# Another column order for the residual xT, and three bias-row copies given to GpSimd

## The reference, cut to what matters

```
x = x + L0(_gn(x))   # layer norm over c; q, k, v, gate; attention over n (16 x 16) for each (a, b), 8 heads;
                     # o = att @ v * sigmoid(gate);  o @ Wo + bo
x = x + L1(_gn(x))   # zn = one norm over everything;
                     # a = sigmoid(lin(zn, W_ga)) * lin(zn, W_la), b likewise with W_gb, W_lb
                     # k = einsum('bitc,bjtc->bijc', a, b); kn = one norm over everything
                     # sigmoid(lin(zn, W_go)) * lin(kn, W_lo)
```

## Time and profile before

| what | value |
|---|---|
| median of three executions | 345.86 us (345.86, 346.84, 344.46) |
| the profiled execution | 347.44 us, of which the span of instructions 345.5 us |
| TensorE's granted clock, mean over the span | 0.897 of full speed |
| busy: PE, PEld, DVE, ACT, POOL | 72%, 44%, 75%, 63%, 57% of the span |
| pipeline of the first block | about 37 to 263 us |
| scalars of the second norm | 263 to 269 us |
| second block up to the final stage | 269 to 320 us |
| final stage and store | 320 to 345.5 us |
| first small matmul behind the wait for B1 (`chsum`) | 264.09 us |
| GpSimd's first `z1_norm`, after 12.9 us idle | 268.69 us |
| first DMA into `bbd[0]` | 282.57 us |
| ScalarE's scaling of unit 7 ends | 328.77 us |

### The profile page before, as it was taken

One profiled execution on the slowest core, in us unless ns is written; L12 is line 12 of the kernel. 1 busy time (PEld: TensorE's weight loads), 2 busy tenths in 40 slices (PEclk: granted clock), 3 DMA queues, 4 the chain that ended last, 5 costly groups with the idle time before them and its releaser, 6 DMA issues.

```text
span 345.5 us, 7455 instructions
## 1 busy us (share of the span) xinstructions
PE 249.6 (72%) x2982; PEld 151.5 (44%) x2982; DVE 258.1 (75%) x466; ACT 217.3 (63%) x392; POOL 195.8 (57%) x169
## 2 busy tenths in 40 slices
PE   0056965599779779679679669769864599998724
PEld 0046342377347346346346347346531145554223
DVE  4985789766797898898898895899796764431972
ACT  4635787389569669669579669468341447567512
POOL 6890564659885896886877843434840862000620
PEclk9995799658998999999999998998997599999856
DMA  7100122013031031031031022100000014667207
GB/s 248 31 0 30 33 63 63 0 39 86 0 93 32 2 92 35 1 93 32 5 88 34 30 64 55 40 0 3 2 2 0 1 30 93 169 183 199 62 0 243
DMA packets 34893, 19.66 MB, mean 57 GB/s; under 512 B 21228, under 2 KB 31788, under 8 KB 34860
## 3 DMA queue, kind: packets, MB, share of 16 engines
q1 hardware_dynamic: 34860, 19.20, 20.7%
HBM read 8.71 MB, written 6.29 MB: 43 GB/s over the span
## 4 chain that ended last, share of the span: by engine, by line
DVE 41%; PE 36%; ACT 14%; issue 7%; DMA 1%; POOL 1%; DVEq 0%; ACTq 0%
PE PS L1126 31%; DVE t_sb L876 6%; DVE nmax L892 5%; DVE S_sb L896 4%; DVE og L869 4%; DVE gn_part L964 3%; DVE sums L820 3%; ACT u_sb L593 2%; ACT PP L623 2%; DVE Z L1113 2%; DVE Z L1117 2%; PE PS L1390 2%; ACT t_sb L607 2%; PE PS L1195 1%; DVE st L830 1%
## 5 line engine op out<-in xcount | busy, mean ns | idle before, releaser
L1126 PE MATMUL PS<-znT,A_bd 128*128 128x512 f16 x192 | 46.9, 387 | 11.8 <-DVE t_sb L876 10.5
L427 POOL TENSOR_TENSOR S_sb<-S_sb,rden 128x512 f32<-128x512 f32 x32 | 35.5, 1133 | 27.7 <-DVE rden L838 27.7
L876 DVE TENSOR_TENSOR t_sb<-PS,t_sb 128x512 f16<-128x512 f32 x64 | 41.1, 683 | 8.6 <-ACT t_sb L607 8.6
L607 ACT CAST t_sb<-PS 128x512 f16<-128x512 f32 x64 | 36.6, 611 | 15.0 <-PE PS L1126 13.5
L613 ACT ACTIVATE S_sb<-S_sb 128x512 f32<-128x512 f32 x32 | 20.2, 631 | 31.8 <-DVE S_sb L896 31.8
L1126 PE MATMUL PS<-zbd,t_sb 128*128 128x64 f16 x768 | 28.9, 199 | 13.6 <-DVE t_sb L876 12.8
L433 POOL TENSOR_TENSOR PP<-S_sb,PP 128x512 f16<-128x512 f32 x28 | 31.8, 1158 | 12.0 <-ACT PP L601 12.0
L1126 PEld LDWEIGHTS PS<-zbd,t_sb 128*128 128x128 f16 x768 | 26.0, 102 | 25.1 <-DVE t_sb L876 16.7
L1126 PE MATMUL PS<-PP,Z 128*128 128x128 f16 x512 | 34.6, 236 | 0.2 <-DVE PP L850 0.2
L593 ACT COPY u_sb<-PS 128x512 f32<-128x512 f32 x64 | 33.7, 626 | 1.6 <-PE PS L1126 1.4
L1126 PEld LDWEIGHTS PS<-znT,A_bd 128*128 128x128 f16 x192 | 16.9, 99 | 40.6 <-DVE t_sb L876 23.9
(11 more groups left out here) (198 smaller groups left out, 529.5 us busy)
## 6 DMA issues: line engine op xcount, KB each, us to landing
Z<-zn_dram SPq DMA_DIRECT2D x64, 64.0 KB, 2.8
x_tok<-in_x SPq DMA_DIRECT2D x4, 512.0 KB, 5.6
zn_dram<-zn_tok SPq DMA_DIRECT2D x8, 256.0 KB, 2.0
zbd<-znT SPq DMA_DIRECT2D x32, 64.0 KB, 2.0
k_dram<-og SPq DMA_DIRECT2D x4, 512.0 KB, 3.6
th<-k_dram SPq DMA_DIRECT2D x16, 128.0 KB, 2.7
out_x<-u_sb SPq DMA_DIRECT2D x4, 512.0 KB, 3.3
PP<-u_sb SPq DMA_DIRECT2D x8, 128.0 KB, 2.4
```

The costliest lines, as they stand in the source:

```text
L427: nc.gpsimd.tensor_tensor(P, P, bcast(rden[:, 32 * k:32 * k + 32], 2, N), ALU.mult).then_inc(p_nrm, 1)
L607: nc.scalar.copy(t_sb[:, HI, :, h], bank_tg(h)[:, :].rearrange("p (q i) -> p q i", i=N)).then_inc(t_hi, 1)
L876: nc.vector.tensor_tensor(t_sb[:, LO, :, h], bank_tg(h)[:, :].rearrange("p (q i) -> p q i", i=N), t_sb[:, HI, :, h], ALU.subtract).then_in ...
L1126: return nc.tensor.matmul(o, l, r, start=start, stop=stop)
```

## The change

The columns of xT are kept in the order (b, n, f) instead of (b, f, n): for one n, the eight values of f are neighbours, and for two n sixteen values are. What follows from it in the code: ScalarE's copy of the transposed x (L692) no longer permutes; the output projection reads `og` permuted, its innermost step being 16 f32 (64 bytes); the two reductions for the statistics run over two axes with an innermost step of one; `z1_norm` reads with other strides of f; and the final additions (L552, L1117) read runs of sixteen. Apart from this, the three copies into `B1` go from VectorE to GpSimd, between its two clears of `bbd`, with waits on `bbd_z` and on `wprep2`.

```diff
--- before.py
+++ after.py
@@ -142,7 +142,7 @@
                .rearrange("p (n c j) -> p n c j", n=4, j=L), x_tok[:, :, :, :].rearrange("p a b c -> p (a b c)").rearrange("p (n c j) -> p n c j", n=4, j=L)]
         gt = [S_sb[:, 4 * k:4 * k + 4].rearrange("p q a n -> p (q a n)")
               .rearrange("p (m c a) -> p m (c a)", a=A2, m=2) for k in range(3)]
-        x1_nfb = xT[:, :].rearrange("p (b f n) -> p b n f", f=A4, n=N)
+        x1_nfb = xT[:, :].rearrange("p (b n f) -> p b n f", f=A4, n=N)
         k_sb = og[:, :, :].rearrange("p h c -> p (h c)")
         kT = th[:, :, :, :].rearrange("p k h c -> p (k h c)")
         tg = Z[:, :, :, :, :, :, :].rearrange("p r f k e d b -> p (r f k e d b)").bitcast(f32)
@@ -256,6 +256,7 @@
 
 
 
+        WPREP2 = 16 + 12 + 1 + 5 + 3
         LZ, LV = 7, 4
         LOOPS = (NS - 4) // 2
         UNITS = (0, 2, 4, 1, 3, 5, 6, 7)
@@ -461,7 +462,7 @@
         def z1_norm(engine, ops, g, done):
 
             for n in range(4 * g, 4 * g + 4):
-                ops.tensor_scalar(z1f[g % 2][:, :, n % 4], xT[:, :].rearrange("p (b f n) -> p f b n", f=A4, n=N)[:, :, :, n],
+                ops.tensor_scalar(z1f[g % 2][:, :, n % 4], xT[:, :].rearrange("p (b n f) -> p f b n", f=A4, n=N)[:, :, :, n],
                                   g2[:, 10, n:n + 1], g2[:, 11, n:n + 1], ALU.mult, ALU.add).then_inc(done, 1)
 
         def z1_low(engine, ops, g, done):
@@ -533,6 +534,13 @@
             for j in range(NS - 1, NS + 2):
                 pool_period(pool, j, j % 2, tail=j <= NS, LN=j < NS - 1)
             nc.gpsimd.memset(bbd[1].rearrange("p n c j -> p (n c j)"), 0.0).then_inc(bbd_z, 1)
+            pool.wait_ge(bbd_z, 1)
+            for r in range(3):
+                pool.wait_ge(wprep2, WPREP2 - 3 + r)
+                row = slice(32 * r, 32 * r + 1)
+                nc.gpsimd.tensor_copy(B1[row, :, :, :, :].rearrange("p k m d e -> p (k m d) e"),
+                                      bcast(b1_s[row, r].rearrange("p k m d -> p (k m d)"), 2, A2)).then_inc(wprep2, 1)
+            pool.wait_ge(wprep2, WPREP2)
             pool.wait_ge(u_mm, 8 * NS)
             nc.gpsimd.memset(bbd[0].rearrange("p n c j -> p (n c j)"), 0.0).then_inc(bbd_z, 1)
 
@@ -689,8 +697,7 @@
                 nc.scalar.copy(x_perm[:, :, e], x_tok[:, e]).then_inc(xp_ok, 1)
             def xT_copy(i):
                 act.wait_ge(xT_mm, i + 1)
-                nc.scalar.copy(xT[:, COLS * i:COLS * i + COLS].rearrange("p (b f n) -> p b f n", f=A4, n=N),
-                               PS[2 + i % 2][:, :].rearrange("p (b n f) -> p b f n", f=A4, n=N)).then_inc(xT_ok, 1)
+                nc.scalar.copy(xT[:, COLS * i:COLS * i + COLS], PS[2 + i % 2][:, :]).then_inc(xT_ok, 1)
             xT_copy(0)
             act.wait_ge(gn_ok, 8)
             nc.scalar.activation(gn_r[:, :], gn_tmp[:, 2], ACT.Sqrt).then_inc(rsq, 1)
@@ -824,12 +831,12 @@
 
             dve.wait_ge(x1_ok, s + 1)
             nc.vector.tensor_reduce(st1[:, 0, bass.ds(s, 1)].rearrange("p s n -> p (s n)"),
-                                    xT[:, bass.ds(s * COLS, COLS)].rearrange("p (q n) -> p n q", n=N),
-                                    op=ALU.add, axis=AX.X).then_inc(x1_st, 1)
+                                    xT[:, bass.ds(s * COLS, COLS)].rearrange("p (b n f) -> p n b f", n=N, f=A4),
+                                    op=ALU.add, axis=AX.XY).then_inc(x1_st, 1)
             dve.wait_ge(x1_sq, s + 1)
             nc.vector.tensor_reduce(st1[:, 1, bass.ds(s, 1)].rearrange("p s n -> p (s n)"),
-                                    sqx[:, :].rearrange("p (q n) -> p n q", n=N),
-                                    op=ALU.add, axis=AX.X).then_inc(x1_st, 1)
+                                    sqx[:, :].rearrange("p (b n f) -> p n b f", n=N, f=A4),
+                                    op=ALU.add, axis=AX.XY).then_inc(x1_st, 1)
 
         def dve_reciprocal(dve, m, half):
             dve.wait_ge(p_sum, 4 * m + 2 * half + 2)
@@ -906,7 +913,6 @@
                                                op0=ALU.add, op1=ALU.add).then_inc(x1_ok, 1)
 
         WP1 = 3 + 4 + 1 + 1
-        WPREP2 = 16 + 12 + 1 + 5 + 3
 
         def dve_weights2(dve):
 
@@ -945,10 +951,6 @@
                     nc.vector.tensor_tensor(b1_r[:, r], rest, b1_s[:, r], ALU.subtract).then_inc(wprep2, 1)
                     n += 1
                     rest = b1_r[:, r]
-            for r in range(3):
-                row = slice(32 * r, 32 * r + 1)
-                nc.vector.tensor_copy(B1[row, :, :, :, :].rearrange("p k m d e -> p (k m d) e"),
-                                      bcast(b1_s[row, r].rearrange("p k m d -> p (k m d)"), 2, A2)).then_inc(wprep2, 1)
             assert n + 3 == WPREP2
 
         def zero(v):
@@ -1227,7 +1229,8 @@
         def pe_out(pe, s):
             for k in range(A2):
                 pe.wait_ge(o_ok, HP * s + k + 1)
-                last = mm(bank_w[D * k:D * k + D], Wo_h[:, :], og[:, k])
+                last = mm(bank_w[D * k:D * k + D], Wo_h[:, :],
+                          og[:, k].rearrange("p (b f i) -> p b i f", f=A4, i=N))
             last.then_inc(w_mm, 1)
 
         def pe_period(pe, j, par, half, B=True, A=True):
```

## The result

| | before | after |
|---|---|---|
| median of 19 executions | 345.2 us (343.12 to 347.61) | 341.35 us (338.05 to 344.65) |
| ratio | 1 | 0.9855, 95% interval 0.9825 to 0.9884 |
| profiled execution: span, mean granted clock | 345.5 us, 0.897 | 340.2 us, 0.946 |

The ratio makes the kernel faster by 1.45%, 5.0 us (4.0 to 6.0) of 345.2; 2.6 us were forecast. It compares fast executions only, all 19 of before and 16 of the 19 of after; the medians of all executions, in the table, give 0.989, 3.85 us. On the prediction's scale (345.86 before) the ratio is 340.8, just under its range, and the medians are 342.0, inside it.

A forecast was written before the change was run, and what follows sets the result against it. No single engine was taken as the bound (VectorE 41% of the chain, TensorE 36%), so each edit was priced where it stands. Gains of 4.2 us less 1.6 lost gave -2.6, from 345.86 to 343.3 us, range 341.0 to 347.2.

The forecast's parts named there:

- the 1.8 us of room: Middle periods: the output projection could end 1.8 us later before VectorE reaches x1, so its 0.8 us longer read hides.
- bounds of 0.1: Second block: ScalarE's copies keep size and length, z1_norm steps over b by 512 bytes either way; zero, 0.1 each way.
- the sum: Whole kernel: all priced terms added, 4.2 us gained and 1.6 us lost, net -2.6 us.
- B1 copies, 1.3 us: Last slab's end: with the copies off VectorE, gate multiplies start at 255.7 instead of 257.0, gaining 1.3 us.
- Statistics, 0.6 at the end and 0.3 in the middle: Reductions fall from 1.02 to 0.68 us: 0.6 gained at the last slab, 0.3 over three middle periods.
- Final adds, 2.0 us: Final stage: adds on neighbouring elements gain 1.2 us on VectorE and 0.8 on GpSimd, all on the path.
- og read with a step, 0.8 us at each end: Output projection: the 64-byte step costs 0.8 us a matmul, hidden in middle periods, 1.6 us lost over the last two slabs' ends.
- An even 0.62 us beside a busy GpSimd: Last slab: gate multiplies reading one PSUM input keep 0.62 us, so the moved GpSimd clear beside them costs nothing.
- (b): Output projection: four strided matmuls take turns at the memory at 1.7 ns an element, 7.0 us; total 376 us; chance 0.08.
- (a): Output projection: TensorE reads the 64-byte step at no cost; total 341.7 us; chance 0.27.
- (c): Output projection: the strided matmuls take turns at the memory, 3.4 us in all; total 347.5 us; chance 0.12.
- (d): Statistics and final adds: reductions over two axes and runs of sixteen are no faster; total 346.2 us; chance 0.08.

The follow-up runs named there:

- the doubled kernel: The changed kernel with og read in neighbouring columns and the four output projection matmuls issued twice in the six middle periods; ratio to before 0.9774.
- the kernel with split weights: The changed kernel with nine of VectorE's twelve low-half weight subtractions moved behind period 8's gate multiplies; ratio to before 0.9796, repeated 0.9778.
- the best version: The changed kernel with the order permuted in PSUM, weight subtractions split around period 8's gate multiplies, and middle-period projection matmuls issued twice; 337.2 us, ratio to before 0.9736.

## Why the prediction was wrong, point by point

The profiled pair, 5.30 us apart, stretch by stretch (us; before to after):

| stretch | forecast | profiled pair |
|---|---|---|
| start to x1 of slab 0 | 0 | -1.53 |
| five middle periods | -0.3 | -3.21 |
| period 8 | +0.8 | +3.13 |
| period 9 | -1.3 + 0.8 | +0.35 |
| last x1 to z1_norm | -0.6 | -0.93 |
| z1_norm to the final stage | 0 | -1.04 |
| final stage and store | -2.0 | -2.07 |
| sum | -2.6 | -5.30 |

- **The step that failed: TensorE's granted clock was taken as unchanged, with no term of its own.** It stands in two places of the prediction. One is the longer projection "in six middle periods it hides in the 1.8 us of room", at nothing; the other is the second block up to the final stage, at zero with bounds of 0.1. (The prediction's last line names moved low stretches as a sign of being wrong, without a price.)
- **The middle.** The longer projection does hide, but it shortens TensorE's wait for x1 from 1.7 to 0.8 us, and two middle periods no longer fall to the lower clock. That is worth 2.7 us: 26.6 and 26.5 us became 25.3 and 25.1 in the two kernels with before's column order and a long projection. The other 0.5 are the statistics.
- **Slab 6's end and period 9.** Without before's low stretch at 233 GpSimd's subtractions are earlier, and VectorE's weights met them: the gate multiplies came 2.3 us later, and the projection ran at the low clock, 0.9. The step itself cost nothing there, 3.71 us with it and 3.71 without (after's row at 240.15 and the doubled kernel's at 239.21). The tail of the same low stretch made period 9 longer by 0.8: its head projection starts 8.6 us behind x1 instead of the 7.8 of before and of the kernel with split weights. So the middle's surplus and the two ends' loss all but cancel: from the first x1 to the last, after is 0.3 us slower than before, where the sum has 0.0. That this stretch fits the forecast is luck.
- **z1_norm to the final stage.** This is the surplus that did not cancel. After z1_norm begins, TensorE stays at the lower clock for 9.1 us in before's profile and for 6.6 in after's. The first ten microseconds from there, before and after:

```profile
268.63:278.63 10.00, 6.77 (x18) 2.34 (x19) 6.87 (x16) 4.13 (x9) 7.45 (x8) 0.55 0.00 1
```

```profile
266.44:276.44 10.00, 6.83 (x23) 2.51 (x23) 7.36 (x19) 4.56 (x11) 7.65 (x9) 0.67 0.00 1
```

The whole difference arises in the first 16 us; from there on VectorE's instructions in this stage lie the same 1.05 us apart, to 0.01. Only 0.13 of it stands 5 us in, while both are still at the lower clock. Over all thirteen profiles the length of this stage, 50.5 to 51.5 us, follows the length of the low stretch, 6.6 to 9.1 us. Whether the change makes it shorter or the execution is not shown: the three kernels with the old order and VectorE's copies have 9.1, 7.8 and 9.0, the ten others 6.6 to 8.5.
- **The start.** Its 1.5 us say nothing of the change: the kernel with the B1 copies alone reaches its first x1 at 101.4 in one profile and at 98.8 in the other, with the same code. Without the start the profiled pair is 3.8 us apart, beside the 3.85 of the medians.
- **How far this goes.** The ratio's 5.0 us (4.0 to 6.0) are about 1 us more than these 3.8; that stays open, the profiles being one execution each.
- **B1 copies, 1.3 us:** right in the kernel with the copies alone (15.1 to 13.8). GpSimd's copies took 0.6 us each, inside the bounds, and nobody waited.
- **Statistics, 0.6 at the end and 0.3 in the middle:** the sizes were right (0.68). From last x1 to z1_norm the layout is worth 0.6 (7.7 to 7.1); the other 0.3 of that stretch are gone in the kernel with the copies alone too, and no run says by what. In the middle four of the five measured periods gained the 0.14 us that the head projection left, and the fifth nothing (25.1 in the old order with a long projection as well), so 0.6 instead of 0.3.
- **Final adds, 2.0 us:** right. From the first multiply to the end of the span 25.4 us became 23.0 to 23.3.
- **og read with a step, 0.8 us at each end:** the price was right: 0.84 where it ran at full clock. Of the forecast's test, 1.9 us for the eight records and x1 at 2.9 us, both numbers came. Net, over whole executions, the step cost 0.6 us (-0.6 to 1.7) in the kernel before, where the sum has 1.6: less, or the same.
- **Two readings.** "An even 0.62 us beside a busy GpSimd" is not in the earlier trace rows, where GpSimd's clear ends at 255.79 and the gate multiplies start at 257.00; after shows it (the clear from 252.87 to 256.38, four multiplies in 2.48 us from 254.89). Rival (b)'s "1.7 ns an element" is less than the 2.0 that 1.02 us for 512 elements gives; with 2.0 it would be worse still.
- **Rivals.** (a), that TensorE doesn't mind the step, has the time (341.7) but not the mechanism: the records show the step's price. (b) and (c) are out: four strided streams side by side took 1.96 us, so they don't take turns. (d) is out.

The Trainium skill (Advanced Engine Details and Errata, SBUF Cachelines) was right for TensorE too: its passes went from 605 to 1052 ns with one hit on a line. By the Trainium skill's page on GpSimd (GPSIMD Engine Reference, Performance pitfalls for Q7 kernels) the pair of adds would have become 0.85 us shorter, an estimate from its cycles for an element; it became 0.47 shorter.

## What to carry to other kernels

Room on TensorE isn't neutral: before pricing a longer or shorter matmul at nothing, look at the granted clock behind the wait that it fills or opens, and compare the periods of a loop one by one, since one low stretch cost 1.3 us of a 25 us period here. When two profiles are compared, lay the low stretches beside the stages first: a stage that the change hardly touches moved by 1 us with them. When one engine gets earlier, look for two-input VectorE instructions that come to stand beside GpSimd's, above all ahead of one that another engine waits for. And where a permutation has to be put somewhere, PSUM's side of a matmul cost nothing here, where SBUF's moving side cost 0.45 us for each pass.

## What the runs showed that I had not expected

- TensorE reading f32 with a step of 64 bytes takes 1052 ns for a pass of 512 columns against 605; four such matmuls still run side by side (eight records in 1.96 us). At the lower clock, behind gate multiplies 0.6 us apart, the four took 3.71 us with the step and without.
- TensorE writing PSUM with a step of 32 bytes: 604 ns, as without.
- Issuing a useless second set of matmuls in a wait made the kernel faster, by 2.8 us of medians in the best version (337.2 against 340.0), every execution faster than every one without.
- Executions of after spread from 338.05 to 344.65 us, the shorter ones mostly with the higher granted clock, so a change worth less than 1% needs many of them: six of the B1 kernel gave 0.9876, twelve more 0.9949.
